# A gated cross-attention and expert block: gate rows spread by DMA, output matrix folded into the values

## The reference

```python
# attention: latents = layernorm(x) without gain
xn, ln = layernorm(ctx, g, b), layernorm(latents, g, b)
q = ln @ Wq.T
kv = concat([xn @ Wkv.T, ln @ Wlkv.T])              # 512 rows of keys and values, 2 heads of 64
attn = softmax(mask(rmsnorm(q) * SCALE @ rmsnorm(k).T))
x = x + tanh(g_xattn) * ((attn @ v) @ Wo.T + bo)
# experts: 32 experts of 64 hidden units, the 4 best gates of a row are kept
xt = layernorm(x)
gates = sigmoid(xt @ expert_sel.T); gate_full = gates where among the top 4, else 0
scores = relu(einsum('nd,edf->nef', xt, keys)) * gate_full[:, :, None]
x = x + tanh(g_ffn) * einsum('nef,efv->nv', scores, values)
```

## Time and profile before

| | |
|---|---|
| median of three runs | 144.35 us |
| the profiled execution's own time | 143.71 us |
| its span in the profile | 141.9 us |
| TensorE busy | 130.3 us, 92% |
| VectorE busy | 105.3 us, 74% |
| ScalarE busy | 72.2 us, 51% |
| GpSimd busy | 9.0 us, 6% |
| moved by DMA | 4.27 MB |

### The profile page before, as it was taken

One profiled execution on the slowest core, in us unless ns is written; L12 is line 12 of the kernel. 1 busy time (PEld: TensorE's weight loads), 2 busy tenths in 40 slices (PEclk: granted clock), 3 DMA queues, 4 the chain that ended last, 5 costly groups with the idle time before them and its releaser, 6 DMA issues.

```text
span 141.9 us, 2125 instructions
## 1 busy us (share of the span) xinstructions
PE 130.3 (92%) x672; PEld 86.3 (61%) x672; DVE 105.3 (74%) x338; ACT 72.2 (51%) x172; POOL 9.0 (6%) x27
## 2 busy tenths in 40 slices
PE   5999696998889997999899999999999999999990
PEld 5958393585445864878556346366545666676860
DVE  1799969597989785986989643945694689769852
ACT  5368675587682763336234451331214666866620
POOL 7970000000000000000000000000000000000000
PEclk9999999599999999999999999999999999999998
DMA  4697000000000000000000000000000000000004
GB/s 92 206 387 330 9 5 0 2 0 0 0 5 0 0 0 2 5 0 0 0 0 0 5 0 0 0 2 0 0 0 0 0 0 0 7 0 0 0 0 148
DMA packets 2170, 4.27 MB, mean 30 GB/s; under 512 B 240, under 2 KB 1648, under 8 KB 1904
## 3 DMA queue, kind: packets, MB, share of 16 engines
q1 hardware_dynamic: 2160, 4.15, 8.5%
HBM read 3.63 MB, written 0.52 MB: 29 GB/s over the span
## 4 chain that ended last, share of the span: by engine, by line
PE 77%; DMA 7%; DVE 5%; issue 3%; SPq 3%; ACT 2%; DVEq 0%; ACTq 0%
PE bank L907 11%; PE bank L727 11%; PE bank L831 9%; PE bank L729 9%; PE bank L728 8%; PE bank L897 7%; DMA values<-values_in 7%; PE bank L762 3%; PE bank L841 3%; PE bank L785 2%; PE bank L758 2%; PE bank L736 2%; PE bank L772 2%; PE bank L814 2%; PE bank L816 1%
## 5 line engine op out<-in xcount | busy, mean ns | idle before, releaser
L541 DVE SCALAR_TENSOR_TENSOR keys<-bank,inT 128x512 f32<-128x512 f32 x32 | 22.0, 689 | 12.3 <-PE bank L729 11.3
L695 ACT ACTIVATE inT<-bank 128x512 f32<-128x512 f32 x32 | 18.5, 595 | 22.8 <-PE bank L897 22.7
L907 PE MATMUL bank<-keys,values 128*128 128x512 f32 x32 | 16.6, 614 | 0.0
L727 PE MATMUL bank<-xm_hi,k_lo 128*128 128x512 f32 x32 | 15.4, 480 | 0.0
L736 PE MATMUL bank<-ident 128*128 128x128 f32 x96 | 13.6, 297 | 1.5 <-POOL ident L303 1.5
L831 PE MATMUL bank<-prob,proj 128*65 128x256 f32 x64 | 15.0, 382 | 0.0
L736 PEld LDWEIGHTS bank<-ident 128*128 128x128 f32 x96 | 12.9, 212 | 1.8 <-POOL ident L303 1.5
L729 PE MATMUL bank<-xm_hi,k_hi 128*128 128x512 f32 x32 | 12.6, 395 | 0.0
L728 PE MATMUL bank<-xm_lo,k_hi 128*128 128x512 f32 x32 | 12.6, 394 | 0.0
L442 DVE CUSTOM_DVE_ANT_0 junk<-bank,mask_b 128x512 bf16<-128x512 f32 x16 | 10.4, 689 | 3.0 <-PE bank L785 3.0
L897 PE MATMUL bank<-gateT,expand 64*128 64x512 f32 x32 | 11.9, 496 | 0.0
(11 more groups left out here) (133 smaller groups left out, 244.7 us busy)
## 6 DMA issues: line engine op xcount, KB each, us to landing
keys<-keys_in SPq DMA_DIRECT2D x1, 1024.0 KB, 8.1
values<-values_in SPq DMA_DIRECT2D x1, 1024.0 KB, 10.1
out<-x_mid SPq DMA_DIRECT2D x4, 128.0 KB, 1.9
wa<-wa_in SPq DMA_DIRECT2D x1, 320.0 KB, 3.5
vecs_x<-x_in SPq DMA_DIRECT2D x1, 256.0 KB, 5.7
cx<-ctx_in SPq DMA_DIRECT2D x2, 96.0 KB, 2.7
cx<-ctx_in SPq DMA_DIRECT2D x1, 192.0 KB, 5.8
wb<-wb_in SPq DMA_DIRECT2D x1, 145.0 KB, 6.1
```

Source lines behind the costliest of these rows:

```text
L541: dve.scalar_tensor_tensor(hid[:, n % 3, :], bank[H_BANK[n % 2]][:, :], 0.0, gated[:, n % 4, :], ALU.max, ALU.mult).then_inc(hid_ready, 1)
L695: act.activation(gated[:, n % 4, :], gates_bank(n)[:, :], ACT.Copy).then_inc(gated_ready, 1)
L727: pe.matmul(o, ll, rh, start=start, stop=False)
L907: last = pe.matmul(bank[ACC_BANK[h]][:, :], values[:, cc], hid[:, n % 3, :], start=(c == 0), stop=(c == EC - 1))
```

## The change

- **Gates.** `spread`, `expand` and ScalarE's copies are gone. The gates are kept once, as 32 rows (`gateT`), and SP writes them, for each batch, to a DRAM scratch `gate_rows` of 32 x 1024. For each chunk SP issues a read of two of these rows, 512 columns, each repeated over 64 partitions, into one of six slots of `gated`, with a semaphore for each slot. A read for slot n waits until `up` n - 6 is done; the writes of batches 2 and 3 come after the reads of half 0 in SP's list. VectorE's `up` waits for its slot.
- **Values.** `fold` multiplies the value weights of each head by the scaled output matrix on the chip (4 fp32 products, a row for the bias). `vlat` and `vctx` multiply the normalized latents and the context by the folded weights, and ScalarE copies that to `vw`, 128 columns and one of ones for each head. `project` makes only queries and keys. `attend` multiplies probabilities (as the stationary operand) by `vw` and so gives the projected output and the sum; `oT` and `out_proj` on TensorE are gone. The probabilities have two buffers.
- **Output.** The result stays transposed, 128 x 1024, and the host turns it. In place of `finish` on TensorE and ScalarE, `turn_res` turns the residual x in the middle of the expert stage.
- **fp32 down.** `WHOLE` is 8: eight chunks are multiplied in fp32, 24 are split.
- **Smaller moves.** The low parts of keys and values go to GpSimd, in four pieces each, which wait for a `row_max` to begin. Some constants go from GpSimd to ScalarE and VectorE, wb is loaded earlier, `norm_qk` and the squares read PSUM directly, queries are turned before keys, `up` has three banks in place of two, `warm` issues one product in place of two. All three lists are written anew.

```diff
-WARM_UP = 2
+WARM_UP = 1
 RING = 4
-WHOLE = 16
+WHOLE = 8
...
+SLOTS = 6
...
 PE_ORDER
...
+    turn_max 2, weights 1.1, weights 2.0, attend 1.0, attend 1.1, turn_mid 0, weights 2.1, row_max 3, attend 2.0,
+    turn_max 3, select 0, turn_mid 1, attend 2.1, weights 3.0, turn_gates 0, select 1, up 0.0, weights 3.1,
+    turn_gates 1, up 0.1, turn_mid 2, attend 3.0, select 2, attend 3.1, turn_res 0, turn_gates 2, up 0.2,
+    turn_res 1, up 0.3, down 0.0, down 0.1, up 0.4, down 0.2, up 0.5, down 0.3, up 0.6, turn_mid 3, down 0.4,
+    up 0.7, select 3, up 0.8, down 0.5, up 0.9, down 0.6, down 0.7, turn_gates 3, up 0.10, up 0.11, up 0.12,
+    up 0.13, down 0.8, down 0.9, up 0.14, down 0.10, up 0.15, down 0.11, down 0.12, up 1.0, up 1.1, up 1.2,
+    down 0.13, down 0.14, up 1.3, up 1.4, up 1.5, down 0.15, turn_res 2, down 1.0, turn_res 3, down 1.1, up 1.6,
+    down 1.2, down 1.3, up 1.7, up 1.8, down 1.4, up 1.9, up 1.10, up 1.11, down 1.5, down 1.6, down 1.7,
+    up 1.12, up 1.13, down 1.8, down 1.9, down 1.10, up 1.14, up 1.15, down 1.11, down 1.12, down 1.13,
...
-        gate = sq[:, 0:2, 0:4, :].rearrange("p i r d -> p i (r d)").rearrange("p i (t q e) -> p i t q e", t=BT, q=4)
-        gateT = sb("gateT", [P, B, S], F32R)
-        gated = inT[:, :, :, :].rearrange("p i b s -> p (i b s)").rearrange("p (i n) -> p i n", i=4)
+        gate = sb("gate", [P, NT, E])
+        gateT = sb("gateT", [E, B, S])
+        gate_rows = nc.dram_tensor("gate_rows", (E, B * S), F32, kind="Internal").ap()
+        gated = inT[:, :, :, :].rearrange("p i b s -> p (i b s)").rearrange("p (i n) -> p i n", i=SLOTS)
...
-        H_BANK, ACC_BANK = (0, 1), (3, 7)
+        H_BANK, ACC_BANK = (0, 1, 2), (3, 7)
...
             sp.dma_start(keys[:, :], keys_in).then_inc(in_keys, 16)
             sp.dma_start(values[:, :], values_in).then_inc(in_values, 16)
+            for h in range(HALF):
+                for b in range(HB * h, HB * h + HB):
+                    sp.wait_ge(gateT_ready, b + 1)
+                    sp.dma_start(gate_rows[:, S * b:S * b + S], gateT[:, b, :]).then_inc(rows_out[h], 16)
+                sp.wait_ge(rows_out[h], 16 * HB)
+                for c in range(EC):
+                    n = EC * h + c
+                    if n == 0:
+                        sp.wait_ge(proj_done, 2 * B)
+                        sp.wait_ge(vlat_done, B)
+                        sp.wait_ge(vctx_done, B)
+                    if n >= SLOTS:
+                        sp.wait_ge(hid_ready, n - SLOTS + 1)
+                    sp.dma_start(gated[:, n % SLOTS, :],
+                                 gate_rows[2 * c:2 * c + 2, HN * h:HN * (h + 1)].unsqueeze(1).to_broadcast([2, F, HN])).then_inc(gated_in[n % SLOTS], 16)
             for b in range(B):
-                t = slice(BT * b, BT * b + BT)
                 sp.wait_ge(res_ready, b + 1)
-                sp.dma_start(out[:, t, :], res[:, t, :]).then_inc(out_done, 16)
+                sp.dma_start(out[:, S * b:S * b + S], res[:, b, :]).then_inc(out_done, 16)
...
+            def low_parts(b, src, hi, lo, hi_ready, lo_ready):
+                pool.wait_ge(max_done, BT * HEADS * b + 1)
+                for q in range(2 * (b % HB), 2 * (b % HB) + 2):
+                    part = slice(QUARTER * q, QUARTER * (q + 1))
+                    pool.wait_ge(hi_ready, q + 1)
+                    pool.tensor_tensor(lo[:, part], src[:, part], hi[:, part].bitcast(F32), ALU.subtract).then_inc(lo_ready, 1)
+            for b in range(HB):
+                low_parts(b, keys, k_hi, k_lo, keys_hi_ready, keys_lo_ready)
+            for b in range(HB, B):
+                low_parts(b, values, v_hi, v_lo, values_hi_ready, values_lo_ready)
 
...
             def up(h, c):
                 n = EC * h + c
 
                 dve.wait_ge(up_done, n + 1)
-                dve.wait_ge(gated_ready, n + 1)
+                dve.wait_ge(gated_in[n % SLOTS], 16 * (n // SLOTS + 1))
                 free_hid(n - 3)
-                dve.scalar_tensor_tensor(hid[:, n % 3, :], bank[H_BANK[n % 2]][:, :], 0.0, gated[:, n % 4, :],
+                dve.scalar_tensor_tensor(hid[:, n % 3, :], bank[H_BANK[n % len(H_BANK)]][:, :], 0.0, gated[:, n % SLOTS, :],
                                          ALU.max, ALU.mult).then_inc(hid_ready, 1)
 
...
+            def fold(i):
+                pe.wait_ge(wo_ready, 1)
+                for a in range(HEADS):
+                    wo = wb[:, B_WO + D * a:B_WO + D * a + D]
+                    pe.matmul(bank[7][:, D * a:D * a + D], wb[:, B_LV + D * a:B_LV + D * a + D], wo, start=True, stop=True)
+                    last = pe.matmul(bank[7][0:DC + 1, D * (HEADS + a):D * (HEADS + a) + D],
+                                     wb[:, B_CV + (DC + 1) * a:B_CV + (DC + 1) * (a + 1)], wo, start=True, stop=True)
+                last.then_inc(fold_done, 1)
+            def vlat(b):
+                pe.wait_ge(fold_ready, 2)
+                pe.wait_ge(inT_ready, 2 * b + 1)
+                if b == 1:
+                    pe.wait_ge(vlat_ready, 1)
+                if b == 3:
+                    pe.wait_ge(vctx_ready, HB)
+                bk = value_bank(b, 0)
+                for t in range(BT):
+                    lat = xnT[:, b, P * t:P * t + P]
+                    for a in range(HEADS):
+                        o = bk[:, D * (HEADS * t + a):D * (HEADS * t + a) + D]
+                        last = pe.matmul(o, lat, folded[:, D * a:D * a + D], start=True, stop=(a > 0))
+                        if a == 0:
+                            pe.matmul(o, wb[:, B_ONE:B_ONE + P], wb[:, B_WO:B_WO + D], start=False, stop=True)
+                last.then_inc(vlat_done, 1)
+            def vctx(b):
+                if b == 0:
+                    pe.wait_ge(row_ready, 1)
+                if b == 1:
+                    pe.wait_ge(vctx_ready, 1)
+                pe.wait_ge(fold_ready, 2)
+                pe.wait_ge(inT_ready, 2 * b + 2)
+                bk = value_bank(b, 1)
+                for t in range(BT):
+                    last = pe.matmul(bk[:, HEADS * D * t:HEADS * D * (t + 1)], cnT[:, b, P * t:P * t + P],
+                                     folded[0:DC + 1, HEADS * D:], start=True, stop=True)
+                last.then_inc(vctx_done, 1)
 
...
-            def attend(b, a):
-                n = HEADS * b + a
-                if n == 0:
+            def attend(b, t):
+                if b == 0:
                     pe.wait_ge(ones_ready, B)
-                pe.wait_ge(prob_ready, 2 * HEADS * b + HEADS + a + 1)
-                for t in range(KT):
-                    last = pe.matmul(head_bank(b, a)[0:DH + 1, 0:S], proj[:, b, t, 4 + a, :], prob[:, a, t, :],
-                                     start=(t == 0), stop=(t == KT - 1))
+                pe.wait_ge(vlat_ready, b + 1)
+                pe.wait_ge(vctx_ready, b + 1)
+                pe.wait_ge(prob_ready, 2 * HEADS * (b + 1))
+                for a in range(HEADS):
+                    for j in range(KT):
+                        last = pe.matmul(bank_of(b, OUT + t)[:, WOA * a:WOA * a + WOA], prob[:, b % 2, a, j, P * t:P * t + P],
+                                         vw[:, b, j, a, :], start=(j == 0), stop=(j == KT - 1))
                 last.then_inc(attend_done, 1)
-            def out_proj(b):
-                if b == 0:
-                    pe.wait_ge(wo_ready, 1)
-                pe.wait_ge(oT_ready, HEADS * (b + 1))
-                for t in range(BT):
-                    for a in range(HEADS):
-                        last = pe.matmul(bank_of(b, OUT + t)[:, WOA * a:WOA * a + WOA], oT[:, b % 2, a, P * t:P * t + P],
-                                         wb[0:DH + 1, B_WO + WOA * a:B_WO + WOA * a + WOA], start=True, stop=True)
-                    last.then_inc(out_done_pe, 1)
 
...
             def up(h, c):
                 n = EC * h + c
                 cc = slice(P * c, P * c + P)
-                if h == 0 and c % 2 == 0:
-                    pe.wait_ge(keys_lo_ready, c // 2 + 1)
+                if h == 0 and c % 4 == 0:
+                    pe.wait_ge(keys_lo_ready, c // 4 + 1)
                 if c == 0:
                     pe.wait_ge(xm_hi_ready, HB * (h + 1))
                     pe.wait_ge(xm_lo_ready, HB * (h + 1))
-                if n < 2:
+                if n == 0:
                     pe.wait_ge(logit_ready, 1)
-                    pe.wait_ge(gate_lo_ready, 2)
-                else:
-                    pe.wait_ge(hid_ready, n - 1)
-                product(bank[H_BANK[n % 2]][:, :], (k_hi[:, cc], k_lo[:, cc]), (half(xm_hi, h), half(xm_lo, h)),
+                elif n == 1:
+                    pe.wait_ge(gateT_ready, 1)
+                elif n == 2:
+                    pe.wait_ge(logit_ready, 2)
+                if n >= len(H_BANK):
+                    pe.wait_ge(hid_ready, n - len(H_BANK) + 1)
+                product(bank[H_BANK[n % len(H_BANK)]][:, :], (k_hi[:, cc], k_lo[:, cc]), (half(xm_hi, h), half(xm_lo, h)),
```

(64 more changed lines are left out.)

358 lines of the change are left out of this document (148 added, 210 removed).

## The result

Median of four runs 246.76 us (246.32 to 248.75), of the kernel before beside it 144.06 (143.42 to 144.61): ratio 1.716, 95% interval 1.703 to 1.728. The profiled execution took 248.75 us, with a span of 246.6; the forecast was 249 for it. Where some runs of a kernel lay in the chip's second, slower state (a lower granted clock and one or two per cent more time), only the others are compared.

A forecast was written before the change was run, and what follows sets the result against it. TensorE bound the kernel before; two-engine gate reads were to replace it. Start to 72.3 us, two halves of 82.4, 2.8 between, 0.6 landing and 6.5 tail gave span 247.0; with 1.8 around it, 249 us, range 232 to 280.

The forecast's parts named there:

- the count of engines: Gate reads from scratch: source's outermost count of 2 leaves two of sixteen DMA engines carrying each read; chance 0.84.
- Price of one chunk: Each gate read: 131,072 B on each of two engines at 25.4 GB/s, 5.15 us; bounds 4.74 and 6.19.
- Start: Before the expert stage: batch 1 gates in SBUF at 69.5 us, written by 71.4, first read's packets at 72.3.
- Half 0: First 16 chunks of the expert stage: 16 x 5.15 = 82.4 us, ending at 154.7 us.
- Between the halves: After chunk 15: row writes of batches 2 and 3 queue behind reads and hold half 1, 2.8 us, to 157.5.
- the prediction's sign: Gate reads in the profile: issue to landing near 6 x 5 us once the queue is full.
- Half 1: Last 16 chunks: 82.4 us again plus 0.6 from last packet to landing, ending at 240.5 us.
- Tail: After the last read: VectorE and ScalarE passes, three matmuls at low clock, residual passes and store, 6.5 us, to 247.0.
- The cover: Expert stage: TensorE's 1.4 us per chunk, 2.8 at low clock, and everything else hide under the 5.15 us transfer.
- The total: Whole kernel: span 247.0 us plus 1.8 around it, 249 us for the profiled execution against 143.71 before.
- Rival 1: Gate reads on all sixteen engines, TensorE stays the bound: span 126, time 128 us, 122 to 134; chance 0.12.
- projections +5.3: Rival 1's sum, TensorE projections with the folded values: 3.5 us per batch after against 2.2, +5.3 over four batches.

The follow-up runs named there:

- experiments 1 to 3: Changed kernel with gate reads split by row: 125.22 us; two, four, eight scratch copies of each row: 167.95, 136.45, 126.34 us; reads cut along columns: 257.98 us.
- experiment 5: Changed kernel with the gate-row writes of batches 2 and 3 issued by ScalarE's queue when ready, not by SyncE: 245.12 us.
- four engines: Changed kernel with each gate row written twice to the scratch, so the read's slowest dimension is 4, not 2: 167.95 us.
- experiment 6: One more matmul per chunk: on the changed kernel 247.92 us; on the kernel with each gate read split by row, 132.52 us against 125.22.
- split read: Changed kernel with each chunk's gate read issued as two transfers, one gate row to 64 partitions each: 125.22 us, ratio 0.872 to the kernel before.

## Why the prediction was right

The whole slowdown hangs on one step, the count of engines, and experiments 1 to 3 show it: with sixteen engines the same change takes 125.22 us. The Trainium skill ("DMA: Bandwidth & Descriptors", "Why a DMA increments its semaphore by 16 and not by 1") gives the number of engines as the largest up to 16 that divides the slowest dimension of both access patterns; here 2, 4, 8, 16 and 64 gave 2, 4, 8, 16 and 16 small packets a read. The steps:

- *Price of one chunk.* Said 5.15 us; measured 5.12.
- *Start.* Gates of batch 1 said to be in SBUF at 69.5; their write was issued at 68.7 and SyncE issued the first read at 70.19, where 71.4 was said. The first read was then used at 77.70, 7.5 us after its issue and not the 6.05 of 0.9 + 5.15: the latency of the end (0.6), counted once at the end of half 1, is here too, and 0.9 more that no run explains. By luck the two errors, 1.2 us early and 1.5 us late, cancel: 77.45 against 77.70.
- *Half 0.* Last `up` at 154.57, said 154.7.
- *Between the halves.* Said 2.8 us more than a chunk, measured 7.65 - 5.12 = 2.53, and shown by experiment 5 to come from the row write. One link was wrong: the read of chunk 15 did not wait for `up 0.9` (123.8 us) but for room in the queue. It was issued at 135.89 and used at 154.57, 18.7 us later, where the prediction's sign was 6 x 5 us from issue to landing. With four engines the extra was 119.90 - 114.90 - 2.56 = 2.44.
- *Half 1.* Last `up` at 239.10, said 240.5.
- *Tail.* Said 6.5 us, measured 246.6 - 239.1 = 7.5. This term was sized too small, and the timeline of the changed kernel shows what it left out:

```profile
239.10 0.69 DVE L527 SCALAR_TENSOR_TENSOR keys<-bank,inT 128x512 f32<-128x512 f32 x1 [4.43 <-DMA inT<-gate_rows]
239.71 0.68 DVE L544 TENSOR_TENSOR hid_lo<-keys,hid_hi 128x512 fp32r<-128x512 f32 x1
...
240.54 0.69 DVE L544 TENSOR_TENSOR hid_lo<-keys,hid_hi 128x512 fp32r<-128x512 f32 x1 [0.15 <-issue]
...
241.96 0.63 PE L703 MATMUL bank<-hid_hi,v_lo 128*128 128x512 f32 x1
...
242.81 0.63 PE L705 MATMUL bank<-hid_hi,v_hi 128*128 128x512 f32 x1
```

VectorE's order has `split 1.14` behind `up 1.15`, so chunk 14's `down` also waits for the last read: six matmuls 0.43 us apart at the 1.2 GHz level stand there, not three, 1.3 us more. They start 0.6 us earlier than said, on chunk 14, while chunk 15 is still being split, and the store took 0.3 more.
- *The cover.* Said to hide everything else; experiment 6 shows it for TensorE, also at the low clock.
- *The total.* That 249 meets 248.75 to 0.3 us is luck: the sum was 1.4 us too long up to the last `up` (240.5 against 239.1) and its tail 1.0 too short, and the other three runs took 246.32 to 247.13.

Rival 1 described the split read, and got 0.12 because the change's source is not split: its sum gave a span of 126.3 and 128 us, the run has 122.4 and 125.22. By its terms: from the first `up` to the last 44.1 us against 59.7 before, so 15.6 less where spreads and `down` were given 16.4; from the last `up` to the end 6.6 against 8.9, 2.3 less where 1.6 were given; and the first `up` at 71.7 against 73.3, 1.6 less where the sum had 2.4 more (projections +5.3, fold +0.9, `out_proj` -3.8). This last is the term that was off: TensorE's busy time up to 72 us did not grow (64.0 us before, 63.7 in the split read, by windows). The rows show two things that the sum left out. Windows of the kernel before, then of the split read, and the products of `warm` in both:

```profile
20.00:40.00 20.00, 17.50 (x107) 11.95 (x106) 16.85 (x51) 13.46 (x39) 0.00 (x0) 0.91 0.00 0
```

```profile
20.00:40.00 20.00, 18.04 (x141) 14.78 (x140) 17.90 (x54) 13.70 (x33) 5.00 (x4) 1.00 0.01 1
```

```profile
L736 PE MATMUL bank<-ident 128*128 128x128 f32 x96 | 13.6, 297 | 1.5 <-POOL ident L303 1.5
```

```profile
L713 PE MATMUL bank<-ident 128*128 128x128 f32 x48 | 8.9, 339 | 1.5 <-POOL ident L314 1.5
```

`warm` issues 48 records fewer, 5.3 us at the 0.11 us of a record, as much as the projections were to add; and the granted clock was 0.91 in 20 to 40 us before, 1.00 in the split read. No run separates the two.
